# A gated cross-attention and expert layer: TensorE's first nine matmuls of constants left out

## Chip, core and metric

The kernel runs on one core of a Trainium2 chip. The metric is the device time of one execution in microseconds (us). The kernel is written by hand: every engine has its own program in a fixed order, and engines wait for each other by semaphores.

## What is computed

x is 4 sequences of 256 tokens, 256 wide (float32). Two steps, cut to the core:

```python
x = x + tanh(g_xattn[0]) * expert_forward(layernorm(x), gate_up_weight, down_weight)
x = x + tanh(g_ffn[0]) * ffn(layernorm(x), w_gate, w1, w2)

def smooth_quant_linear(x, w):            # int8 product; maxima per column, then per row
    s = sqrt(max(abs(x), axis=0) / max(abs(w), axis=0))
    xs, ws = x / s, w * s
    x_scale, w_scale = rowmax(abs(xs)) / 127, rowmax(abs(ws)) / 127
    return round(xs / x_scale) @ round(ws / w_scale).T * x_scale * w_scale.T
def expert_forward(x, guw, dw):           # once for each of the 4 sequences
    gate, up = split(smooth_quant_linear(x, guw))
    return smooth_quant_linear(silu(gate) * up, dw)
# ffn: each token goes to the best of 8 experts, 128 places each:
#   out = combine(gelu(dispatched @ w1[e]) @ w2[e]), w1[e] 256x1024, w2[e] 1024x256
```

## The kernel before

There are two stages. In the first (to some 55 us) the four sequences b = 0 to 3 go through the quantised layer, staggered over the engines. In the second the eight experts run one after another.

At the start, SyncE issues the loads of x (`load_x`) and of the gate and up weights cw (`load_cw`) in the order x0, x1, cw0, x2, cw1, x3, cw2, cw3. What follows for one sequence:

- VectorE takes the row statistics of x (`stats1`), GpSimd makes the reciprocal deviation (`rstd1`), ScalarE normalises (`norm1`) into `rows_w`.
- TensorE turns the weights (`turn1w(b)`, four 128x128 float32 transposes of cw[b], line 1019) and the normalised rows (`turn1(b)`, four transposes of rows_w, the same line). Both write to the PSUM tile bk[b], one half each.
- VectorE takes column maxima out of PSUM: `amax1w(b)` (line 715) of the turned weights, `amax1(b)` (lines 721 to 725) of the turned rows, and their ratio. GpSimd makes the scales from it with a power (`root_1(b)`, lines 368 and 370).
- ScalarE scales (`scale1`, line 531), TensorE turns back (`turn2`, line 1048), VectorE takes row maxima (`scales1`, line 740), ScalarE quantises, GpSimd rounds, TensorE turns (`turn3`, bfloat16 transposes of `ints`, line 1084) and multiplies.

Once, between `turn1(1)` and `turn1w(3)`, TensorE runs `mean_w` (line 1070, the column means of w_gate, four records in the trace), and VectorE centres with it (`centre_w`, line 780, tile wgc). VectorE's program has `amax1w(2)`, `amax1(1)`, `amax1(2)` behind `centre_w`, and TensorE's `turn1w(3)` waits for wgc.

`fill(b, a, n)` (line 1010) runs n bfloat16 matmuls of constants (`upper` against `identb`, 512 columns) into a half of a PSUM tile bk[b]. Nothing reads what they leave there: the next step that uses the half writes it anew. They stand in seven places of TensorE's program: 6 ahead of `turn1w(0)`, 3 ahead of `turn1w(1)`, 2 ahead of `turn2(0, 1)`, 4 ahead of `turn2(1, 1)`, and 6, 2 and 2 later in the first stage (25 in all). All have line 1013 in the trace. Transposes have one record each; a float32 matmul that is no transpose has two.

In the second stage TensorE works through `hidden` (line 1182) and `expert_out` (lines 1194 and 1196).

Of the kernel before, what the change touches and what calls it, by code (L numbers as in the profile page):

```python
# [5 lines left out]
def gated_smoothquant_moe_kernel(nc, x_in, ctx_in, down_in, g_xattn, g_ffn, w_gate, w1, w2, scratch, out):  # L6
# [20 lines left out]
    B, T, D = x_in.shape  # L27
    I = down_in.shape[2]
    E, _, F = w1.shape
    J = T // P  # L30
    K = D // P
# [14 lines left out]
    with ctx:  # L46
# [960 lines left out]
        def _(pe):  # L1007
            pe.wait_ge(consts, 4)

            def fill(b, a, n):  # L1010

                for _ in range(n):
                    nc.tensor.matmul(bk[b][:, a, :], upper[:], identb[:].unsqueeze(1).to_broadcast([P, 4, P]),  # L1013
                                     start=True, stop=True)
# [8 lines left out]
            def turn1w(b):  # L1023

                pe.wait_ge(cw_here[b], 16)
                if b == B - 1:
                    pe.wait_ge(wgc_ready, 1)
                turn1_half(b, 1, cw).then_inc(t1w_ready, 1)
# [185 lines left out]
                                           start=(n == 0), stop=(n == NF - 1))  # L1214
                ins.then_inc(y_used, 1)

            fill(3, 0, 6)
            turn1w(0)
            fill(3, 0, 3)
            turn1w(1)  # L1220
            turn1(0)
            turn1w(2)
# [96 lines left out]
```

## Time and profile before

| | us |
|---|---|
| median of 3 runs | 116.8 (116.26 to 116.91) |
| the profiled execution | 117.76 |
| its span, first to last instruction | 116.0 |
| around the span | 1.76 |
| TensorE matmul busy | 98.6 (85% of the span) |
| VectorE busy | 86.7 (75%) |
| ScalarE busy | 72.3 (62%) |
| GpSimd busy | 56.0 (48%) |
| share of the chain that ended last on TensorE, GpSimd, VectorE | 50%, 16%, 14% |

Start times below count from the first instruction. Matmul records overlap each other: the pace of a group is read from the distance between starts, not from the duration of one. "x4" behind a row means that four instructions are merged into it, and its duration runs from the first's start to the last's end.

### The profile page before, as it was taken

The numbers are of one execution on the slowest core, as the hardware profiler recorded it, in microseconds if no ns is written. First come the engines' busy times: TensorE is split into PE (matmuls) and PEld (weight loads), VectorE is DVE, ScalarE is ACT, GpSimd is POOL, SyncE is SP. The second block draws the span as 40 slices with busy tenths as digits, with TensorE's granted clock in tenths as the row PEclk, the third lists the DMA queues.
The fourth block names the chain that finished last, engine by engine and source line by source line (L and its number), as shares of the span: only waits on it lengthen the run. The fifth ranks groups of instructions, "written<-read, shape, count | busy, mean of one in ns | idle before, by whom it ended". The sixth has DMA issues, their size and how long they took to land.

```text
span 116.0 us, 2229 instructions
## 1 busy us (share of the span) xinstructions
PE 98.6 (85%) x741; PEld 84.4 (73%) x741; DVE 86.7 (75%) x231; ACT 72.3 (62%) x154; POOL 56.0 (48%) x119
## 2 busy tenths in 40 slices
PE   0948868997986898996889999999999999999930
PEld 0227546996845667874689989899999989899820
DVE  6646897999997889682318698999898696939450
ACT  4073579798797899966018564998573739376000
POOL 7855598787969849878670000426030303011041
PEclk9999999999999999999999999999999999999998
DMA  3899998999990942409932999989898860101011
GB/s 108 255 353 291 240 172 291 323 363 353 378 328 26 292 149 94 160 25 237 346 103 66 292 398 353 309 214 408 303 330 280 298 236 10 45 0 51 0 45 45
DMA packets 16218, 24.86 MB, mean 214 GB/s; under 512 B 1368, under 2 KB 13913, under 8 KB 15184
## 3 DMA queue, kind: packets, MB, share of 16 engines
q1 hardware_dynamic: 15440, 22.65, 62.1%
q0 software_dynamic: 768, 2.08, 4.8%
q8 instruction: 6, 0.10, 0.3%
q14 instruction: 4, 0.03, 0.1%
HBM read 20.50 MB, written 4.28 MB: 214 GB/s over the span
## 4 chain that ended last, share of the span: by engine, by line
PE 50%; POOL 16%; DVE 14%; issue 6%; DMA 6%; SPq 2%; ACT 2%; POOLq 1%
PE bk L1182 25%; PE bk L1194 11%; PE bk L1196 6%; DMA cw<-in_ctx_gu 6%; POOL slot_rows L426 4%; POOL row L412 2%; DVE am L740 2%; PE bk L1168 2%; POOL sc L370 2%; DVE am L786 2%; PE bk L1155 2%; PE bk L1208 2%; PE bk L1019 1%; SPq L231 1%; DVE am L721 1%
## 5 line engine op out<-in xcount | busy, mean ns | idle before, releaser
L494 POOL DMA_INDIRECT out<-scrow,gr x8 | 9.5, 1182 | 43.1 <-DVE scrow L961 41.7
L1182 PE MATMUL bk<-rows_w,w_sb 128*128 128x128 f32 x192 | 23.0, 275 | 0.5 <-ACT rows_w L583 0.5
L1182 PEld LDWEIGHTS bk<-rows_w,w_sb 128*128 128x128 f32 x192 | 22.2, 192 | 0.8 <-ACT rows_w L583 0.7
L1194 PE MATMUL bk<-w2p,hh 128*128 128x512 f32 x56 | 20.3, 403 | 0.0
L862 DVE TENSOR_TENSOR w2p<-w_sb,w2p 128x1024 fp32r<-128x1024 f32 x12 | 14.1, 1217 | 3.8 <-POOL begun L482 2.7
L1196 PE MATMUL bk<-w2p,hl 128*128 128x256 f32 x56 | 15.6, 278 | 0.0
L597 ACT ACTIVATE w2p<-w_sb 128x1024 fp32r<-128x1024 f32 x12 | 12.0, 1054 | 5.3 <-PE bk L1196 5.3
L661 ACT ACTIVATE hh<-bk 128x512 fp32r<-128x512 f32 x16 | 9.5, 595 | 4.7 <-PE bk L1182 4.7
L1194 PEld LDWEIGHTS bk<-w2p,hh 128*128 128x128 f32 x56 | 10.5, 188 | 2.1
L1196 PEld LDWEIGHTS bk<-w2p,hl 128*128 128x128 f32 x56 | 10.5, 188 | 0.0
L874 DVE TENSOR_TENSOR hl<-wide_a,hh 128x512 fp32r<-128x512 f32 x16 | 10.4, 683 | 0.0
L1013 PE MATMUL bk<-identb,upper 128*128 128x512 bf16 x25 | 7.8, 438 | 3.0 <-POOL upper L308 3.0
L426 POOL DMA_INDIRECT slot_rows<-row,slot x8 | 8.7, 1090 | 2.9 <-issue 2.9
L663 ACT ACTIVATE wide_a<-bk 128x512 f32<-128x512 f32 x16 | 9.6, 598 | 0.0
L1155 PE MATMUL bk<-row,wide_b 128*128 128x258 f32 x32 | 7.9, 391 | 1.8 <-POOL row L415 1.8
L1155 PEld LDWEIGHTS bk<-row,wide_b 128*128 128x128 f32 x32 | 5.8, 190 | 2.9 <-issue 2.2
L531 ACT ACTIVATE wide_a<-bk,sc 128x256 f32<-128x256 f32 x14 | 5.4, 482 | 2.3 <-POOL sc L370 2.3
L513 ACT ACTIVATE rows_w<-x,sh,rs 128x256 f32<-128x256 f32 x6 | 3.3, 593 | 5.3 <-POOL sh L333 5.3
L540 ACT ACTIVATE wide_b<-bk,q1r 128x256 f32<-128x256 f32 x16 | 6.4, 494 | 0.0
L1013 PEld LDWEIGHTS bk<-identb,upper 128*128 128x128 bf16 x25 | 2.5, 107 | 5.0 <-POOL upper L308 3.0
L1048 PE MATMUL bk<-ident,wide_a 128*128 128x128 f32 x32 | 4.5, 281 | 1.0 <-ACT wide_a L531 0.9
L1048 PEld LDWEIGHTS bk<-ident,wide_a 128*128 128x128 f32 x32 | 3.4, 140 | 2.5 <-ACT wide_a L531 2.4
(164 smaller groups left out, 229.9 us busy)
## 6 DMA issues: line engine op xcount, KB each, us to landing
w_sb<-in_w SPq DMA_DIRECT2D x12, 1024.0 KB, 7.4
slot_rows<-empty SPq DMA_DIRECT2D x1, 1068.0 KB, 9.9
x<-in_x SPq DMA_DIRECT2D x4, 256.0 KB, 4.3
cw<-in_ctx_gu SPq DMA_DIRECT2D x4, 256.0 KB, 6.3
cw<-in_w SPq DMA_DIRECT2D x1, 1024.0 KB, 7.1
out<-row SPq DMA_DIRECT2D x4, 256.0 KB, 2.6
x<-in_w SPq DMA_DIRECT2D x1, 1024.0 KB, 5.8
wide_a<-in_w SPq DMA_DIRECT2D x1, 1024.0 KB, 6.7
```

The costliest lines, as they stand in the source:

```text
L426: nc.gpsimd.indirect_dma_start(scratch, bass.IndirectOffsetOnAxis(ap=slot[:, b, j:j + 1], axis=0), row[:, b, j, 0:ROW], None, bounds_check ...
L494: nc.gpsimd.indirect_dma_start(out_rows, bass.IndirectOffsetOnAxis(ap=gr[:, e, TOKEN:TOKEN + 1].bitcast(I32), axis=0), yo[:, e % 2, :], No ...
L597: last = nc.scalar.activation(w2p[:, e % 2, n:n + NF // 2, 0], w2v[:, n:n + NF // 2], ACT.Copy)
L661: nc.scalar.activation(hh[:, e % 2, part].rearrange("p n c -> p (n c)"), HB[e % 2][:, m, :], ACT.Gelu_apprx_tanh).then_inc(hhigh_ready, 1)
L663: nc.scalar.activation(hs[:, e % 2, part].rearrange("p n c -> p (n c)"), HB[e % 2][:, m, :], ACT.Gelu_apprx_tanh).then_inc(gelu_ready, 1)
L862: last = nc.vector.tensor_tensor(w2p[:, e % 2, part, 1], w2v[:, part], w2p[:, e % 2, part, 0].bitcast(F32), ALU.subtract)
L874: nc.vector.tensor_tensor(hl[:, e % 2, part], hs[:, e % 2, part], hh[:, e % 2, part].bitcast(F32), ALU.subtract).then_inc(hlow_ready, 1)
L1013: nc.tensor.matmul(bk[b][:, a, :], upper[:], identb[:].unsqueeze(1).to_broadcast([P, 4, P]), start=True, stop=True)
L1155: ins = nc.tensor.matmul(XD[e], hot[:, b, j, e * C:(e + 1) * C], row[:, b, j, 0:RSTD + 1], start=(b == 0 and j == 0), stop=(b == B - 1 and ...
L1182: ins = nc.tensor.matmul(HB[e % 2][:, m, n * C:(n + 1) * C], wv[:, k, o:o + P], xgT[:, e % B, k], start=(k == 0), stop=(k == K - 1))
L1194: nc.tensor.matmul(YB[e % 2], hh[:, e % 2, n], w2p[:, e % 2, n].rearrange("p a d -> p (a d)"), start=(n == 0), stop=False)
L1196: ins = nc.tensor.matmul(YB[e % 2][:, 0:D], hl[:, e % 2, n], w2p[:, e % 2, n, 0], start=False, stop=(n == NF - 1))
```

## The change

The two calls of `fill` ahead of `turn1w(0)` and `turn1w(1)` are gone; the other 16 matmuls of constants stay. Nothing else differs.

```diff
-            fill(3, 0, 6)
             turn1w(0)
-            fill(3, 0, 3)
             turn1w(1)
             turn1(0)
             turn1w(2)
```

On TensorE, the start of the program. The names are bk for the PSUM tiles, identb and upper for the constants, cw for the gate and up weights, rows_w for the normalised rows, wide_a for the scaled ones. Before:

```order
0 L1006 UNCONDITIONAL_BRANCH
1 L1013 MATMUL bk<-identb,upper 128x512 x6
2 L1019 MATMUL bk<-ident,cw 128x128 x4
3 L1013 MATMUL bk<-identb,upper 128x512 x3
4 L1019 MATMUL bk<-ident,cw 128x128 x4
5 L1019 MATMUL bk<-ident,rows_w 128x128 x4
6 L1019 MATMUL bk<-ident,cw 128x128 x4
```

and now, with four rows more:

```order
0 L1006 UNCONDITIONAL_BRANCH
1 L1019 MATMUL bk<-ident,cw 128x128 x8
2 L1019 MATMUL bk<-ident,rows_w 128x128 x4
3 L1019 MATMUL bk<-ident,cw 128x128 x4
4 L1019 MATMUL bk<-ident,rows_w 128x128 x4
5 L1070 MATMUL bk<-wg,spread 128x8 x2
6 L1019 MATMUL bk<-ident,cw 128x128 x4
7 L1019 MATMUL bk<-ident,rows_w 128x128 x4
8 L1013 MATMUL bk<-identb,upper 128x512 x2
```

The turnings of cw[0] and cw[1] now follow each other as TensorE's first work; behind them the order is what it was. The other engines' programs are the same in both.

## Rows read from the trace of the kernel before

**Rows 1.** Chain that ended last: start us, us, what. From the weights' loads on.

```profile
3.65 6.48 DMA cw<-in_ctx_gu
...
10.18 1.09 PE bk L1019 x8
11.27 0.47 PE bk L1070 x4
...
11.77 0.17 DVE wgc L780
11.94 0.60 DVE am L715
...
14.13 1.02 POOL sc L370
...
19.49 0.64 PE bk L1019 x4
```

**Rows 2.** Timeline of TensorE's matmuls, 3 to 19 us; idle time and releaser in brackets.

```profile
3.01 2.74 PE L1013 MATMUL bk<-identb,upper 128*128 128x512 bf16 x6 [3.01 <-POOL upper L308]
5.78 0.66 PE L1019 MATMUL bk<-ident,cw 128*128 128x128 f32 x4
6.27 0.81 PE L1013 MATMUL bk<-identb,upper 128*128 128x512 bf16 x3
8.74 0.66 PE L1019 MATMUL bk<-ident,cw 128*128 128x128 f32 x4 [1.66 <-DMA cw<-in_ctx_gu]
9.23 0.60 PE L1019 MATMUL bk<-ident,rows_w 128*128 128x128 f32 x4
10.18 0.66 PE L1019 MATMUL bk<-ident,cw 128*128 128x128 f32 x4 [0.34 <-DMA cw<-in_ctx_gu]
...
11.12 0.61 PE L1070 MATMUL bk<-wg,spread 128*128 128x8 f32 x4
...
12.99 0.59 PE L1013 MATMUL bk<-identb,upper 128*128 128x512 bf16 x2
...
14.89 1.03 PE L1013 MATMUL bk<-identb,upper 128*128 128x512 bf16 x4
16.81 2.11 PE L1048 MATMUL bk<-ident,wide_a 128*128 128x128 f32 x16 [0.89 <-ACT wide_a L531]
```

**Rows 3.** Timeline of TensorE's weight loads inside the first six fills.

```profile
3.84 0.15 PEld L1013 LDWEIGHTS bk<-identb,upper 128*128 128x128 bf16 x1 [0.28 <-issue]
4.26 0.15 PEld L1013 LDWEIGHTS bk<-identb,upper 128*128 128x128 bf16 x1 [0.28 <-issue]
```

**Rows 4.** Timelines of VectorE and of GpSimd: the waits behind TensorE's first turnings.

```profile
6.47 0.69 DVE L715 TENSOR_REDUCE am<-bk 128x2 f32<-128x512 f32 x1 [1.37 <-PE bk L1019]
7.95 0.75 DVE L706 BATCH_NORM_STATS2 st<-x 128x6 f32<-128x256 f32 x2 [0.79 <-DMA x<-in_x]
...
11.77 0.17 DVE L780 TENSOR_TENSOR wgc<-wg,bk 128x16 f32<-128x16 f32 x1 [0.45 <-PE bk L1070]
...
13.83 0.22 POOL L368 TENSOR_SCALAR ra<-ra 128x2 f32<-128x2 f32 x1 [1.08 <-DVE ra L725]
```

**Rows 5.** Busy time of each engine in stretches, granted clock and DMA.

```profile
core 0: us, PE busy (x) PEld busy (x) DVE busy (x) ACT busy (x) POOL busy (x), PEclk, DMA share, GB/s
3.00:5.70 2.70, 2.69 (x6) 0.72 (x6) 1.82 (x8) 0.11 (x1) 2.39 (x9) 1.00 0.82 250
15.95:19.45 3.50, 2.11 (x16) 1.71 (x16) 3.38 (x10) 3.50 (x11) 3.01 (x8) 1.00 0.95 231
22.00:30.00 8.00, 7.28 (x73) 6.87 (x72) 7.69 (x26) 7.19 (x20) 6.90 (x15) 1.00 1.00 349
60.00:80.00 20.00, 20.00 (x162) 19.23 (x161) 16.92 (x30) 14.53 (x23) 3.47 (x4) 1.00 0.83 276
115.00:116.00 1.00, 0.00 (x0) 0.00 (x0) 0.00 (x0) 0.00 (x0) 0.00 (x0) 0.50 0.00 0
```

**Rows 6.** Timeline of TensorE: bfloat16 transposes of one sequence (turn3).

```profile
24.73 0.61 PE L1084 MATMUL bk<-identb,ints 128*128 128x128 bf16 x8
```

## The prediction

> **What bounds the kernel now.** I read the chain of waits first, because it says at which point TensorE's pace at the start begins to matter. Up to 10.13 us the chain is a transfer: cw[2] is issued at 3.65 and its landing releases TensorE [rows 1]. From there it is TensorE (eight transposes from 10.18, then `mean_w` from 11.27), VectorE (`centre_w` at 11.77, then the maxima), GpSimd's powers, and so on without another transfer. So whatever TensorE does before 8.7 us is free as long as it is done by then, and what it does from 10.18 to 11.7 is on the path that sets the end. The reader is to see two waits there: VectorE stood still 0.45 us for `mean_w`, and GpSimd 1.08 us for the ratio that VectorE makes after it [rows 4]. Neither has other work to slide in, since each program's order is fixed. In the second stage TensorE has no free time at all, 20.00 of 20 us [rows 5]; it can't win back a late start.
>
> Then the timeline of TensorE. The fills that go are the six from 3.01 and the three from 6.27 [rows 2]. They end, by these rows, at 5.75 and 7.08; the work behind them starts at 5.78 and 8.74.
>
> Last the clock. The granted clock reads 1.00 from 3.00 to 5.70 [rows 5], but the rows of the fills speak against that reading for this stretch: their weight loads stand 0.42 us apart [rows 3], which for 512 columns is the lower level, 1.2 GHz. From 6.27 on the fills are at the higher: four take 1.03 us and two 0.59 [rows 2], so one more costs (1.03 - 0.59) / 2 = 0.22 us. Between them the clock went from 1.2 to 2.4 GHz, with TensorE at work back to back since 3.01. I take 5.7 us for it, since the four transposes at 5.78 need 0.49 us to the next start, exactly as the four at 8.74 do (to 9.23).
>
> **The change part by part.**
>
> *The fills' own time.* 2.74 + 0.81 = 3.55 us of TensorE's work goes [rows 2]. All of it lies beside transfers: behind the last fill TensorE waits 1.66 us for cw[1]. Value: 0. If the first six did hold up `turn1w(0)`, the reader of it, VectorE, would start earlier than 6.47, but it waits 0.79 us for x[2] before 7.95 anyway [rows 4]. Still 0.
>
> *`turn1w(0)` at the lower clock.* Four transposes take 0.49 us at the higher level. No row shows a transpose at the lower one. The fills there take 0.42 against 0.22, a factor of 1.9; the other bound is a factor of 1, if something else than the array's clock paces a transpose. I take nearly the full factor, 0.24 for 0.1225, because the bfloat16 transposes follow the higher clock: eight take 0.61 us in all, at most 0.076 each [rows 6], less than the 0.107 that 128 columns take at 1.2 GHz. `turn1w(0)` then ends some 0.5 us later; VectorE's idle 0.79 us ahead of x[2] covers it. Cost 0. Without that cover it would cost 0.5.
>
> *`turn1w(1)`, `turn1(0)`, `turn1w(2)`, `turn1(1)`, `mean_w`.* With the fills gone, TensorE has done only four transposes when it comes to 8.74, and stood idle for 2 us behind them, so I expect it at 1.2 GHz there. Sixteen transposes lead up to `mean_w`. Before, they took from 8.74 to 11.12 with waits for transfers of 0.34 us among them. At the lower clock TensorE is behind the transfers and doesn't wait: 8.74 + 16 x 0.24 = 12.58. That is 1.46 us later than 11.12. `mean_w` itself, 0.47 us on the chain [rows 1], has four weight loads and few columns: between 0 and another 0.47. With no rise of the clock until then, the sum is 1.5 to 1.9 us.
>
> When does it rise? The earliest that I allow is with as much unbroken work behind it as in the trace, 3.01 to 5.7, thus 8.74 + 2.7 = 11.4. By then 2.7 / 0.24 = 11 transposes are done and 5 are left, 0.6 us: `mean_w` starts at 12.05, 0.9 us later. So the path at `centre_w` moves by 0.9 us (early rise) to 1.9 us (none yet). I take 1.3, a little under the middle of the two; the trace has one rise only, and nothing says that the next needs exactly as much.
>
> *What hangs on it.* VectorE goes from `centre_w` at 11.77 into `amax1w(2)` at 11.94 and on; GpSimd has waited 1.08 us for the ratio before its power at 14.13, and the chain leads by way of GpSimd to `turn1(3)` at 19.49 without a transfer [rows 1, 4]. With no transfer on it, I let the shift go through one to one. The two fills at 12.99 and the four at 14.89 each wait on TensorE's order only; if they run at the lower clock they cost 6 x 0.2 = 1.2 us more, ahead of `turn2(1, 1)` at 16.81, which now has 0.89 us of idle time in front [rows 2]. With a rise by about 12.5 that is none.
>
> Sum against the profiled execution: 117.76 + 0 + 0 + 1.3 = 119.1 us. The runs without a profile have a median of 116.8, 0.96 less; the same 1.3 gives **118.1 us**.
>
> A page speaks against a sum of this size. The Trainium skill, "TensorE: Matmul & The Clock Gate", Part 1, states that the array is at half rate by default and released by activity, and that the ramp's penalty is under 1% of a typical kernel's span. The first half fits the fills' spacing of 0.42 and then 0.22; by the second the change would cost under 1.2 us, against the 0.9 to 1.9 from the rows. I keep the rows, since this kernel is short and has the transposes on its path.
>
> **The rivals.**
>
> *Transposes don't raise the clock (late rise), 118.8 to 120.3.* If only products lift it, it stays low through `mean_w`'s few columns and past the transposes until the six fills left have run. Cost: 1.9 at `centre_w`, then `turn2(0)` and the fills at the lower level: from 13.0 the work of `turn1w(3)`, `turn1(2)`, two fills, `turn2(0)`, four fills is 16 x 0.24 + 6 x 0.42 = 6.4 us from about 14.0, to 20.4 against the 16.81 of before, less what the rise gives back on the way. 2 to 3.5 us in all, 118.8 to 120.3. Against it: from 15.95 to 19.45 TensorE does transposes alone and the clock stays at 1.00 [rows 5], while after the last matmul it is 0.50 at 115. That shows that they hold the clock, not that they raise it. The same page, Part 4, says that full clock does not engage for transpose mode; [rows 6] contradict it as to speed. Chance 0.18.
>
> *The clock stays low for much of the first stage, 121 to 124.* From 22 to 30 us TensorE is busy 7.28 of 8 us at the higher clock [rows 5]; at half of it, this stretch alone would add some 4 to 7 us. It decides if the fills that stay are too sparse to lift it. I see no reason why transposes and real products, nearly without a gap, should leave it low. Chance 0.06.
>
> *Not slower, 116.8 to 117.3.* The mechanism is the pace of a float32 transpose. If it is set by the weight load or by issue (each takes 0.1225 us where a bfloat16 one takes at most 0.076), the sixteen transposes keep their starts at either clock, TensorE still waits for cw[2], and all that is left is `mean_w`, up to 0.47 us. It decides at a pace of about 0.14 us: sixteen of these are 2.2 us, and `mean_w` could start at 11.12 as before. The same result comes if the clock is up by 8.74 all the same. Against it: the fills, whose pace did double, are matmuls like them, and the transposes of bfloat16 do run faster than 1.2 GHz allows. Chance 0.15.
>
> *Faster, below 116.2.* Fewer weight reads beside the first transfers could bring cw[2] in earlier; the constants are small and nothing in the trace shows such a contention. Chance 0.03.
>
> **How the numbers follow.** Forecast 0.58 (117.7 to 118.7), late rise 0.18, low for long 0.06, not slower 0.15, faster 0.03. The predicted time is the forecast's, 118.1. The range is 117.2 to 119.9: it takes in the forecast with both ends of its bounds and most of the late rise, and leaves out most of "not slower", "faster", the top of the late rise and "low for long", together about 0.2. A measurement of this kernel can tell 0.5%, 0.6 us, from no change. Slower by more than that: 0.58 + 0.18 + 0.06 less some 0.02 for small costs = 0.80; within it 0.17; faster 0.03.
>
> **What would show it right or wrong.** In the profile after: (1) the four transposes at about 5.8 and those at 8.74 have starts 0.24 us apart, not 0.12, and the granted clock reads 0.50 there or has no reading; (2) TensorE has no wait for cw[2] at 10.2; (3) `mean_w` starts between 12.0 and 12.6, and `centre_w` at 12.7 to 13.6 instead of 11.77; (4) GpSimd's power for b = 1 starts 0.9 to 1.9 us after 14.13; (5) the clock rises between 11.4 and 13, or else the fills behind 13 are 0.42 apart (late rise); (6) the first `hidden` starts later by the same amount. If the transposes are still 0.12 apart at 8.74 the forecast is wrong, and "not slower" is right. If (1) to (4) hold but the end moves by much less than `centre_w` does, then "one to one" was the wrong step.

## Result and profile after

Slower, by less than forecast. In the first comparison the changed kernel has a median of 117.38 us against 116.69 (20 runs each), a ratio of 1.0059 (95% interval 1.0035 to 1.0084). Two further comparisons gave 1.0086 (1.0048 to 1.0123) and 1.0079 (1.0045 to 1.0112). Over all its 38 executions the median is 117.52, over the 118 of before 116.67: 0.85 us or 0.7%, where 1.3 us was forecast and 117.2 to 119.9 stated as range. The spread grew as well: 111 of 118 executions of before are under 117.5 us, but 19 of 38 of the changed kernel.

The ratios leave out executions that are more than 1.5% above a kernel's fastest, so where many are left out the median of all of them stands beside the ratio.

The page of the changed kernel, against a span of 116.0 before:

```profile
span 115.2 us, 2212 instructions
PE 96.6 (84%) x732; PEld 85.0 (74%) x732; DVE 86.6 (75%) x231; ACT 72.3 (63%) x154; POOL 56.0 (49%) x119
PEclk9999999999999999999999999999999999999995
```

The profiled execution of the changed kernel is *shorter* than the one of before that the prediction stands on (116.94 against 117.76 us), though its median is longer. So a difference of two profiles alone would have told the wrong sign. TensorE's timeline tells why; these rows answer to [rows 2]:

```profile
5.86 1.09 PE L1019 MATMUL bk<-ident,cw 128*128 128x128 f32 x4 [5.86 <-DMA cw<-in_ctx_gu]
7.29 1.12 PE L1019 MATMUL bk<-ident,cw 128*128 128x128 f32 x4 [0.34 <-DMA cw<-in_ctx_gu]
8.20 1.06 PE L1019 MATMUL bk<-ident,rows_w 128*128 128x128 f32 x4
9.05 1.06 PE L1019 MATMUL bk<-ident,cw 128*128 128x128 f32 x4
9.91 0.65 PE L1019 MATMUL bk<-ident,rows_w 128*128 128x128 f32 x4
10.39 0.51 PE L1070 MATMUL bk<-wg,spread 128*128 128x8 f32 x4
```

Three things are to be seen. The four transposes of a group take 1.06 to 1.12 us where they took 0.60 to 0.66, and from one group to the next it is 0.85 us where it was 0.45 to 0.49. Taken singly, the starts of transposes in a row stand 0.213 us apart here, at the lower clock, and 0.109 us in before; only the first two of a group that follows a wait are farther apart (up to 0.27 and 0.17 us). In the fourth of the groups from 7.29 on this ends (0.65, and 0.48 to `mean_w`); the trace's first entry of a granted clock, at the full 2.4 GHz, is at 10.00 us. And the weights cw[1] were there at 7.3 us, not at 8.7; the wait for cw[2] (0.34 us in [rows 2]) is gone.

VectorE and GpSimd, answering to [rows 4]:

```profile
6.99 0.69 DVE L715 TENSOR_REDUCE am<-bk 128x2 f32<-128x512 f32 x1 [1.91 <-PE bk L1019]
7.59 0.74 DVE L706 BATCH_NORM_STATS2 st<-x 128x6 f32<-128x256 f32 x2
...
10.94 0.17 DVE L780 TENSOR_TENSOR wgc<-wg,bk 128x16 f32<-128x16 f32 x1 [0.35 <-PE bk L1070]
...
13.00 0.22 POOL L368 TENSOR_SCALAR ra<-ra 128x2 f32<-128x2 f32 x1 [0.99 <-DVE ra L725]
```

The first reduction is 0.52 us later than before and is hidden, as said: the statistics of x[2] follow it, at 7.59. `centre_w` still waits for TensorE, and GpSimd for VectorE.

The chain of waits, answering to [rows 1]; all sixteen transposes now stand in it as one piece:

```profile
2.66 4.58 DMA cw<-in_ctx_gu
...
7.29 3.26 PE bk L1019 x16
10.55 0.36 PE bk L1070 x4
...
10.94 0.17 DVE wgc L780
...
13.30 1.02 POOL sc L370
...
18.66 0.64 PE bk L1019 x4
```

From the start of `mean_w` to the end of the span it is 116.0 - 11.12 = 104.9 us in [rows 2], and 115.2 - 10.39 = 104.8 here. That quantity is the ruler of all that follows.

### The profile page after: what moved, and what is told of

It reads as the page before. It is cut to its first block, busy times and chain, and to the rows that moved or that the text cites. A ratio compares the mean times of both kernels' runs of the same rounds, so it can differ in the third digit from the quotient of the medians.

```text
span 115.2 us, 2212 instructions
## 1 busy us (share of the span) xinstructions
PE 96.6 (84%) x732; PEld 85.0 (74%) x732; DVE 86.6 (75%) x231; ACT 72.3 (63%) x154; POOL 56.0 (49%) x119
## 4 chain that ended last, share of the span: by engine, by line
PE 53%; POOL 16%; DVE 14%; issue 6%; DMA 4%; ACT 2%; SPq 1%; POOLq 1%
PE bk L1182 25%; PE bk L1194 11%; PE bk L1196 6%; POOL slot_rows L426 4%; DMA cw<-in_ctx_gu 4%; PE bk L1019 3%; POOL row L412 3%; DVE am L740 2%; PE bk L1168 2%; POOL sc L370 2%; DVE am L786 2%; PE bk L1155 2%; PE bk L1208 2%; DVE am L721 1%; POOL ints L398 1%
## 5 line engine op out<-in xcount | busy, mean ns | idle before, releaser
L1019 PE MATMUL bk<-ident,cw 128*128 128x128 f32 x16 | 3.9, 391 | 6.6 <-DMA cw<-in_ctx_gu 6.2
L1019 PEld LDWEIGHTS bk<-ident,cw 128*128 128x128 f32 x16 | 2.7, 201 | 7.0 <-issue 6.2
```

What stands on the lines that cost most here:

```text
L1019: ins = nc.tensor.transpose(bk[b][:, a, k * T + j * P:k * T + (j + 1) * P], src[:, b, j, k * P:(k + 1) * P], ident[:])
```

## Experiments

Each kernel was profiled once and timed beside the kernel before on the same chip. The table has what all of them gave; the rise is the first entry of 2.4 GHz in the trace's granted clock.

| kernel | cw[1] turned from | rise | `mean_w` at | span | span - `mean_w` | median (before) | ratio |
|---|---|---|---|---|---|---|---|
| before | 8.74 | 5.74 | 11.12 | 116.0 | 104.9 | 116.69 | |
| after | 7.29 | 10.00 | 10.39 | 115.2 | 104.8 | 117.38 (116.69) | 1.0059 |
| before_again | 7.67 | 8.62 | 9.89 | 114.8 | 104.9 | 116.63 (116.50) | 1.002 |
| after_again | 7.64 | 11.84 | 11.11 | 116.3 | 105.2 | 117.71 (116.50) | 1.0086 |
| before_third | 7.15 | 5.92 | 9.66 | 114.5 | 104.8 | 116.48 (116.66) | 0.9991 |
| after_third | 7.41 | 10.80 | 10.85 | 115.6 | 104.8 | 117.44 (116.66) | 1.0079 |
| no_six | 7.53 | 10.19 | 10.61 | 115.5 | 104.9 | 117.34 (116.50) | 1.0065 |
| no_three | 7.67 | 6.09 | 10.20 | 115.1 | 104.9 | 117.21 (116.50) | 1.0013 |
| narrow | 7.48 | 10.91 | 10.94 | 115.7 | 104.8 | 118.01 (116.56) | 1.0135 |
| early_ten | 7.41 | 5.26 | 9.97 | 114.9 | 104.9 | 116.64 (116.56) | 1.0006 |
| before_late | 8.67 | 11.97 | 12.03 | 116.8 | 104.8 | 117.46 (116.56) | 1.0078 |
| after_late | 7.95 | 17.03 | 11.42 | 116.9 | 105.5 | 118.59 (116.56) | 1.018 |
| before_swap | 7.67 | 7.62 | 10.15 | 114.6 | 104.4 | 116.58 (116.83) | 0.9983 |
| after_swap | 7.70 | 17.14 | 11.17 | 116.8 | 105.6 | 117.60 (116.83) | 1.0016 |
| early_ten_swap | 7.19 | 5.75 | 9.67 | 114.2 | 104.5 | 116.02 (116.66) | 0.9946 |
| no_fifteen | 7.09 | 9.96 | 10.27 | 115.8 | 105.5 | 118.14 (116.83) | 1.0135 |
| no_fills | 7.11 | 11.27 | 10.63 | 117.0 | 106.4 | 119.22 (116.83) | 1.0174 |

### The two kernels again

> The kernel before, run once more to see how its start differs between executions. Theory A (the transfers' landing differs by execution, whatever the fills do): the second transposes of gate and up weights need not start at 8.74 us; they start anywhere from 7.2 to 8.8, and mean_w accordingly at 9.9 to 11.2 us, still at 0.12 us a transpose. Theory B (the fills themselves keep the transfers back): again 8.6 to 8.8 us and a landing median of 6.3 us for cw. Ratio to the kernel before 1.000 by both.

> The changed kernel once more. Theory A: ratio to before 1.003 to 1.009 as measured, transposes from the second group on 0.21 us apart until the clock rises somewhere from 9.5 to 13 us; where the landings are late (8.7 us), mean_w starts later than the 10.39 us of the first profile, about 12 us. Theory B: landings early (7.3 us for cw[1]) once more, since the fills are gone.

before_again, TensorE's timeline:

```profile
3.00 2.74 PE L1013 MATMUL bk<-identb,upper 128*128 128x512 bf16 x6 [3.00 <-POOL upper L308]
5.54 1.06 PE L1019 MATMUL bk<-ident,cw 128*128 128x128 f32 x4
6.39 1.49 PE L1013 MATMUL bk<-identb,upper 128*128 128x512 bf16 x3
7.67 1.06 PE L1019 MATMUL bk<-ident,cw 128*128 128x128 f32 x4
8.53 0.65 PE L1019 MATMUL bk<-ident,rows_w 128*128 128x128 f32 x4
9.02 0.60 PE L1019 MATMUL bk<-ident,cw 128*128 128x128 f32 x4
9.45 0.60 PE L1019 MATMUL bk<-ident,rows_w 128*128 128x128 f32 x4
9.89 0.51 PE L1070 MATMUL bk<-wg,spread 128*128 128x8 f32 x4
```

Its chain of waits:

```profile
3.00 2.74 PE bk L1013 x6
5.75 0.85 PE bk L1019 x4
6.60 1.28 PE bk L1013 x3
7.88 0.87 PE bk L1019 x4
...
8.77 0.69 DVE am L715
```

This is the kernel *with* its fills, and the clock was still low at 7.67: the fills of 6.39 take 1.49 us instead of 0.81, and `turn1w(1)` 1.06. The rise comes at 8.62 here against 5.74 in the first profile, though TensorE's program to that point is the same. When the clock rises differs from execution to execution. And the three fills, slow, ended where `turn1w(1)` begins, without a wait for a transfer: they had held it back. The chain says the same of all nine: it starts with the constants and goes through the fills and `turn1w(1)` to VectorE, past `mean_w`, and `centre_w` at 10.57 had no wait in front. The groups at 9.02 and 9.45, at the higher clock, start 0.43 us apart: 0.109 us a transpose. So the landing fell where theory A put it, but not the "0.12 us a transpose" that came with it.

after_again, the same view:

```profile
7.64 1.12 PE L1019 MATMUL bk<-ident,cw 128*128 128x128 f32 x4 [1.40 <-DMA cw<-in_ctx_gu]
...
10.26 1.06 PE L1019 MATMUL bk<-ident,rows_w 128*128 128x128 f32 x4
11.11 0.86 PE L1070 MATMUL bk<-wg,spread 128*128 128x8 f32 x4
```

Here all sixteen transposes ran low, 3.47 us from 7.64 to 11.11, and `mean_w` took 0.86 instead of 0.51. The landings vary on both kernels. The loads of cw took 4.5 us in the median in before_again and 4.6 in before_third, with the fills, 4.8 to 5.2 us in the changed kernel's three profiles, without them, and 6.3 us in the first profile of before only. Theory B (the fills hold the transfers back) falls.

> The kernel before, a third profile. If the late landing of its first profile (second group of transposes at 8.74 us) was that execution's own, they start at 7.5 to 7.9 us here and mean_w at 9.8 to 10.3; if it belongs to the kernel, at 8.6 us or later.

> The changed kernel, a third profile and more times, to settle the size between the 0.7 and the 1.2 us of the two comparisons. By the terms as measured so far: second group at 7.1 to 7.7 us, mean_w 3.1 to 3.5 us later, 104.9 us from there to the end if the clock is up by then and up to 105.6 if not; median 0.7 to 1.2 us over before.

```profile
7.15 0.66 PE L1019 MATMUL bk<-ident,cw 128*128 128x128 f32 x4 [0.18 <-DMA cw<-in_ctx_gu]
7.65 0.60 PE L1019 MATMUL bk<-ident,rows_w 128*128 128x128 f32 x4
8.54 0.66 PE L1019 MATMUL bk<-ident,cw 128*128 128x128 f32 x4 [0.29 <-DMA cw<-in_ctx_gu]
...
9.66 0.52 PE L1070 MATMUL bk<-wg,spread 128*128 128x8 f32 x4
```

These are before_third's rows: high clock, cw[1] at 7.15, both earlier than expected. The first profile's 8.74 is the latest of the seventeen profiles, among those without an added transfer by 1.0 us: it belongs to that execution. after_third turned cw[1] at 7.41 and reached `mean_w` at 10.85, 3.44 us later, as expected.

### One group of fills at a time

```diff
-            fill(3, 0, 6)
             turn1w(0)
             fill(3, 0, 3)
```

> Only the six fills ahead of turn1w(0) left out; the three behind it stay. Clock theory: the three run at the lower clock, 0.43 us apart, to about 8.0 us, and the rise comes by 8 to 11 us, earlier than without all nine: between no cost and the full one, ratio 1.000 to 1.006; the fills may also hold the second transposes back by some 0.7 us where the weights land early. If the fills only kept transfers back, ratio below 1.000.

1.0065 (1.0041 to 1.0089), median 0.84 us over before: like the whole change, and just above the 1.006 that was expected at most. The three fills run low and end where `turn1w(1)` begins (this is no_six):

```profile
5.99 1.49 PE L1013 MATMUL bk<-identb,upper 128*128 128x512 bf16 x3
7.53 1.12 PE L1019 MATMUL bk<-ident,cw 128*128 128x128 f32 x4
```

```diff
             fill(3, 0, 6)
             turn1w(0)
-            fill(3, 0, 3)
```

> Only the three fills behind turn1w(0) left out; the six stay. Clock theory: in executions where the six have raised the clock it stays up over the idle time to 7.3 or 8.7 us and nothing is lost: ratio 0.999 to 1.003, transposes 0.12 us apart at the second group in most executions. If both groups were needed, the ratio is that of the whole change, 1.006.

The profile has the clock up (rise 6.09) and the groups at 7.67 and 8.16 start 0.49 us apart as at the higher clock, which is what the clock theory says. But the times fall into two lots: seven of twelve between 116.2 and 117.4 us, four at 118.2 to 118.5, and one far off (344). The ratio of 1.0013 (0.998 to 1.0046) leaves the second lot out; the median of all, 117.21, is 0.7 us above before. That six fills alone raise the clock in some executions only, and that the slow lot is the one where they missed, is likely from the sizes but not shown: the one profile is of the fast lot.

### Columns, or a place in the program

```diff
-            fill(3, 0, 6)
+            narrow(3, 0, 6)      # matmul(bk[b][:, a, 0:E], upper[:], identb[:, 0:E])
             turn1w(0)
-            fill(3, 0, 3)
+            narrow(3, 0, 3)
```

> The nine matmuls of constants stay in number and place but have 8 columns instead of 512, so that TensorE does next to nothing in the same places. Clock theory (the fills' columns raise the clock): like the changed kernel, ratio 1.005 to 1.009, the second transposes 0.21 us apart. Rival (what counts is that TensorE's program starts early or that instructions stand there): like the kernel before, ratio 1.000 to 1.002.

1.0135 (1.0091 to 1.0179) in six runs. Nine matmuls in the same places, but of 8 columns, bring nothing:

```profile
3.00 0.33 PE L1019 MATMUL bk<-identb,upper 128*128 128x8 bf16 x6 [3.00 <-POOL upper L308]
...
7.48 1.12 PE L1024 MATMUL bk<-ident,cw 128*128 128x128 f32 x4 [0.29 <-DMA cw<-in_ctx_gu]
```

The rival is out: it is the work of the fills that counts. The ratio is above the 1.005 to 1.009 expected, though the profile is that of a changed kernel (`mean_w` at 10.94). The six times fall into two lots, 117.34 to 117.54 and 118.48 to 118.92 us. The changed kernel has times in both too, but its fastest is 116.53, so that the ratio leaves out what lies above 118.3; here nothing is left out. That, and six runs only, may be all that the difference is.

### More fills, earlier

```diff
+            nc.vector.memset(ones[:], float(E)).then_inc(ones_ready, 1)   # VectorE's first instruction
-            pe.wait_ge(consts, 4)
-            fill(3, 0, 6)
+            pe.wait_ge(ones_ready, 1)
+            for _ in range(10):
+                nc.tensor.matmul(bk[3][:, 0, :], ones[:], ones[:].unsqueeze(1).to_broadcast([P, 4, P]),
+                                 start=True, stop=True)
+            pe.wait_ge(consts, 4)
```

> More heat, earlier: the six fills are replaced by ten of another constant that VectorE writes first, from about 1.2 us to 5.5 us; the three stay. Clock theory: the clock has risen by 6 us in more executions than before, none pays at the second transposes; median 0.1 to 0.4 us below the kernel before and a narrower spread, ratio 0.996 to 0.999, mean_w at 9.8 to 10.3 us. Rival (the kernel before loses nothing to the clock): 1.000.

1.0006 (0.9985 to 1.0026): no gain, where 0.996 to 0.999 was expected. The clock was up early (5.26), but then TensorE waits 0.19 and 0.38 us for cw[1] and cw[2] and `mean_w` starts at 9.97. With the clock up, the landings set its start, and before_again, low until 8.62, was there at 9.89 with earlier landings. What before loses to a late rise is too small to be seen in the median of these twelve runs.

### The landings

```diff
             load_cw(0)
+            sp.dma_start(w2_sb[:, 2, 0:J * D]..., x_in[0]...).then_inc(early_here, 16)
             load_x(2)
```

> The kernel before with one more transfer of 256 KB (read by nobody) ahead of x[2] and cw[1], so that they land some 0.7 us later, as in the first profile of before. The start of mean_w moves by as much, and the end with it: 0.5 to 1.0 us slower than before, ratio 1.004 to 1.009. If the end doesn't hang one to one on mean_w, less.

> The changed kernel with the same extra transfer. Theory A (late landings make the change dearer or cheaper): the difference to before_late is clearly other than the 0.7 to 1.2 us between the two without it. Theory C (the price hangs on sixteen transposes of 0.21 instead of 0.12 us and on when the clock rises, not on the landings): again 0.6 to 1.2 us over before_late, ratio to before 1.010 to 1.018.

The medians are 117.46 and 118.59, 0.90 us over before and 0.88 over after_again's 117.71. The difference between the two is 1.13 us, inside 0.6 to 1.2: in the medians, of six runs each, theory C holds and later landings move both alike. The two profiles don't show it: their spans are 116.8 and 116.9, and before_late's is its slowest execution. In it the three fills at the lower clock stood between a late cw[0] and `turn1w(1)` at 8.67, and all sixteen transposes ran nearly as slowly as in the changed kernel; nothing was left of the fills' gain. The two profiles are of use for the clock:

```profile
10.38 1.06 PE L1024 MATMUL bk<-ident,cw 128*128 128x128 f32 x4
11.23 0.96 PE L1024 MATMUL bk<-ident,rows_w 128*128 128x128 f32 x4
12.03 0.51 PE L1075 MATMUL bk<-wg,spread 128*128 128x8 f32 x4
```

These are before_late's: a kernel with all its fills whose clock rose at 11.97 only. after_late's rose at 17.03:

```profile
11.42 0.86 PE L1075 MATMUL bk<-wg,spread 128*128 128x8 f32 x4
12.64 1.09 PE L1024 MATMUL bk<-ident,cw 128*128 128x128 f32 x4 [0.35 <-DVE wgc L785]
```

Its span is 116.9 - 11.42 = 105.5 behind the start of `mean_w`, 0.6 us above the ruler. Of that 0.35 is `mean_w` itself; another five microseconds at the lower clock cost 0.3. So with VectorE's order as it is, the price of the clock is paid ahead of `mean_w`, and hardly behind it.

### Is VectorE's wait for mean_w on the path?

```diff
             amax1(0)
-            centre_w()
             amax1w(2)
+            centre_w()
             amax1(1)
```

> VectorE takes the maxima of the turned weights of sequence 2 (line 715) ahead of centre_w (line 780) instead of behind it; nothing else. If its wait of 0.45 us for mean_w is on the path that sets the end, the reduction fills that wait and all behind moves up by 0.3 to 0.6 us: ratio 0.995 to 0.998. If the path goes elsewhere: 1.000, or slower, since turn1w(3) waits longer for wgc.

> The same swap on the changed kernel. If the price of the change is paid through mean_w and centre_w, the swap takes 0.3 to 0.6 us off it as well: ratio to before 1.002 to 1.005 instead of 1.006 to 1.009. If the low clock is paid elsewhere (in turn2, or later), it stays at 1.006 to 1.009.

before_swap's profile shows it (VectorE), the reduction of line 715 now in what was a wait:

```profile
10.17 0.68 DVE L715 TENSOR_REDUCE am<-bk 128x2 f32<-128x512 f32 x1
10.80 0.17 DVE L780 TENSOR_TENSOR wgc<-wg,bk 128x16 f32<-128x16 f32 x1
10.89 0.68 DVE L721 TENSOR_REDUCE am<-bk 128x2 f32<-128x512 f32 x1
```

From `mean_w` to the end it is 104.4 instead of 104.9, some 0.4 us less. The times can't tell it by themselves (0.9983, 0.9956 to 1.0009). after_swap is undecided: a ratio of 1.0016 (0.9979 to 1.0053) without its four longest runs, a median 0.77 us over before with them. One of the four (118.54) is the profiled one. Its clock rose at 17.14 only, and 105.6 us lie behind `mean_w`, 1.2 more than in before_swap; after_late, with a rise as late, had 0.6 more than the ruler. The chain goes through TensorE all the way from `centre_w`, and six of the fills that stayed are on it:

```profile
12.38 1.94 PE bk L1019 x8
14.32 0.85 PE bk L1013 x2
15.18 1.71 PE bk L1048 x8
16.88 1.05 PE bk L1013 x4
```

With VectorE's wait filled, a low clock behind `mean_w` was no longer nearly free.

> Ten earlier fills of another constant and the swap of centre_w with the maxima of sequence 2 together. With the clock up by 6 us the start hangs on the landings and then on VectorE; the swap fills its wait: ratio 0.994 to 0.998. If the swap gave nothing in the kernel before, 1.000.

Both together gave a median of 116.02 against 116.66, 0.9946 (0.9922 to 0.9969), two runs far off left out: faster than both kernels. Its profile has again 104.5 us behind `mean_w` (114.2 - 9.67). Alone neither edit is clear of no change (1.0006 for the earlier fills, on another chip, and 0.9983 for the swap). With the 0.4 us that both profiles show, the wait is on the path, though how the gain divides between the two edits stays open.

### The fills that stayed

```diff
-            fill(3, 0, 2)
             turn2(0, 1)
             turn2(0, 0)
-            fill(3, 0, 4)
             turn2(1, 1)
```

(both on the changed kernel; no_fills leaves out the last ten as well)

> The changed kernel with the two fills ahead of turn2(0, 1) and the four ahead of turn2(1, 1) left out too. If the transposes raise the clock, these six are not needed: ratio as the changed kernel, 1.005 to 1.010, rise from 9.5 to 13.5 us in most executions. If transposes count little, the rise comes behind 17 us and the ratio is 1.010 to 1.030.

> All 25 matmuls of constants left out. If the clock, once up, holds through the first stage without them: as no_fifteen, within 0.002. If the later ten are what holds it, the clock falls between 35 and 55 us, and part of the first stage or the first expert runs at 1.2 GHz: 1 to 3 us more.

The rise came as without the change, at 9.96 and 11.27. But the clock fell again. Granted clock is the third value from the end; first no_fifteen, then no_fills:

```profile
10.00:16.70 6.70, 4.00 (x32) 3.23 (x31) 5.97 (x20) 4.83 (x13) 4.75 (x9) 1.00 1.16 206
16.90:20.10 3.20, 3.20 (x17) 2.98 (x16) 2.27 (x6) 3.08 (x9) 2.82 (x7) 0.50 0.98 335
```

```profile
35.20:38.50 3.30, 3.06 (x13) 2.65 (x14) 1.51 (x7) 1.68 (x6) 3.22 (x9) 0.50 0.27 72
```

Before the fall in no_fifteen, at 16.78, TensorE had turned sixteen tiles from 11.13 on with idle time among them, the last of it 1.74 us up to 15.85, and then some eight more. In no_fills it stood idle for 2.37 us at the same place and the clock stayed up; it fell at 35.16, in a gap of some 2 us where six of the fills had been. Afterwards it rose again, at 20.20 and 38.57.

The ratios are 1.0135 (1.0089 to 1.0182) and 1.0174 (1.011 to 1.0238), and the profiles have 0.7 and 1.5 us more behind `mean_w` than the ruler. So no_fifteen came out above the 1.005 to 1.010 expected, though its interval touches it, and no_fills took its second branch, a fall between 35 and 55 us. It is not only the profiled executions: the mean granted clock is 0.985 or less in three of six executions of no_fifteen and in five of six of no_fills; of the changed kernel's 38 executions none is under 0.988. So the fills that stayed help to keep the clock up.

## Why the prediction was right or wrong

**The clock is what the fills buy: right.** Signs (1) and (2) came: the transposes run slower from 5.8 us on, and the wait for cw[2] is gone. The granted clock has no reading of 0.50 before its first entry and shows 1.00 there, as in [rows 5]; the pace has to be read from the rows. Signs (3) to (6) were times set against the first profile of before, and missed: `mean_w` at 10.39, GpSimd's power at 13.30 and the first `hidden` at 57.70 (58.53 there) are *earlier* than there, and the clock rose at 10.00. Held against before_third (9.66), `mean_w` is later by 0.7 us. narrow shows that it is the fills' columns, not their place.

**A shift of mean_w goes through one to one: right.** Twelve profiles have VectorE's order unchanged and the later fills in place. In ten of them 104.8 or 104.9 us lie behind the start of `mean_w`, over starts from 9.66 to 12.03; in the two whose clock was still low there (after_again, after_late) it is 105.2 and 105.5. The six fills behind it cost nothing at either clock that these profiles had (0.3 us at most, in after_late). The rule has a floor that the prediction doesn't name: in before_again `mean_w` started early enough that VectorE came to `centre_w` without a wait. And it is shown for this order of VectorE's only: in after_swap 1.2 us were paid behind `mean_w`.

**turn1w(0) hidden: right.** Its reader moved by 0.52 us, and the idle time before x[2] took it.

**The size: wrong, 1.3 us instead of 0.85 (0.69 in the first comparison).** The step that failed is the price of the sixteen transposes: "8.74 + 16 x 0.24 = 12.58", and no rise allowed before 11.4. Measured, a transpose takes 0.213 us at the lower clock, and the rise came at 10.00 to 11.84. Four points of the sum were off.

- *The pace.* "I take nearly the full factor, 0.24 for 0.1225". The factor was right: 0.213 against 0.109 is 1.96, where the fills have 0.427 against 0.216. The 0.1225 was wrong. It is the mean of a group that follows a wait, whose first step is longer (0.17 us); the next group in [rows 2], from 10.67 to 11.12, already reads 0.45 us for four. Sixteen at the lower clock took 3.47 us (after_again) instead of 3.84. That alone takes 0.4 us off the "no rise" end: 3.47 against 2.38 from 8.74 to 11.12 is 1.1, not 1.46; with `mean_w`'s 0.35 (of "between 0 and another 0.47") the upper end is 1.4, not 1.9.
- *The rise.* I allowed nothing before 11.4. It came at 10.00, 10.80 and 11.84 in the three profiles, 2.7, 3.4 and 4.2 us after the second group's start; counted from that start, the earliest case that I allowed is the first of the three, but its time on the clock was wrong. The three profiles of the changed kernel need 3.10, 3.44 and 3.47 us for the sixteen. Against the 2.38 of before that is 0.7 to 1.1 us, and with up to 0.35 for `mean_w` 0.7 to 1.4, where the prediction had 0.9 to 1.9.
- *The base.* "Before, they took from 8.74": I took one execution's landings as the kernel's. In before_again and before_third `mean_w` starts at 9.89 and 9.66, 1.2 to 1.5 us earlier. By the medians of before_late and after_late it shifts both kernels alike and so costs the difference little, but it hid the next term, and it made a profile of 117.76 us out of a kernel of 116.7.
- *"Value: 0" for the fills' own time.* With weights landing at 7.1 to 7.7 us, three fills at the lower clock (1.49 us, before_again and no_six) end just where `turn1w(1)` begins. Where the fills miss the rise they are on the path, all nine of them in before_again's chain, and the changed kernel gets something back: it turned cw[1] from 7.29, 7.64 and 7.41, and before_again from 7.67. That is 0 to 0.4 us by these starts; how much it is in the mean isn't shown.

In starts of `mean_w`: 10.39, 11.11 and 10.85 in the changed kernel, against 9.89 and 9.66 where the weights weren't late. That is 10.78 - 9.78 = 1.0 us on the mean of so few profiles, against 0.85 in the medians of 38 and 118 executions. How often the fills of before miss the rise, and so how the 0.85 divides between executions, stays open: it would take many profiles of one kernel.

**The rivals.** *Transposes don't raise the clock*: out as a mechanism. Up to 10.00 us the changed kernel's TensorE had done nothing but transposes, and the clock rose. That speaks against the Trainium skill, "TensorE: Matmul & The Clock Gate", Part 4, where full clock is said not to engage for transpose mode. The same page of the Trainium skill, in Part 1, has the ramp's penalty under 1% of a typical kernel's span; the three comparisons agree, with 0.6 to 0.9%. But a late rise as this rival describes it does happen. In after_late and after_swap the clock rose at 17.03 and 17.14 only, when two of the fills that stayed had run, 0.43 us apart, and the other four had begun. With the 1.1 us of the sixteen transposes that makes some 1.7 us in after_late, less than the rival's 2 to 3.5. That the changed kernel's four longest executions (118.35 to 118.71 us) are such ones is likely, but none of them was profiled. Against this rival the prediction also said that transposes hold the clock. That was more than its row could show: in no_fifteen, with transposes and gaps only behind `mean_w`, it fell. *Low for much of the first stage*: not with the fills that stayed; a first step of it shows when they go (no_fifteen, no_fills). *Not slower* by the pace of a transpose: out, the pace nearly doubles, as the fills' does. *Faster*: out; the loads of cw took no less time without the fills.

## What to carry to other kernels

A warm-up of TensorE is worth the work that would otherwise run at half the clock on the path, and no more: here sixteen transposes by 0.104 us, less the wait for a transfer in which the faster pace ends (0.34 us in [rows 2]) and less what a rise midway gives back. Price it from the first transfer that releases real work to the first point where another engine waits for TensorE; behind that point, five microseconds at the lower clock cost 0.3 us here. That depends on what fills the other engine's wait: in after_swap, with the wait filled, a rise as late cost about twice as much behind that point (1.2 us against 0.6, `mean_w` itself included). Take the pace of an instruction from a run of them in a row, not from a group of four behind a wait. And where a kernel begins on transfers, take two or three profiles before one execution's landing times go into a sum: here they differed by more than the change was worth.

## What the runs showed of the hardware

- The clock's rise is not fixed to the program. With the same instructions it came at 5.74, 5.92 and 8.62 us (three profiles of before), and in before_late, with six fills from 3.00, at 11.97. In the three profiles of the changed kernel the execution's time goes with it: rise at 10.00, 10.80, 11.84 us, time 116.94, 117.38, 118.07 us. The landings of cw[1] differ too (7.29, 7.41, 7.64), by 0.35 of the 1.1 us; the rest goes with the rise. Some of what looks like noise in the runs is likely this.
- A clock once up can fall in a stage in which TensorE still works but with gaps, and rise again: 0.50 in the row 16.90 to 20.10 of no_fifteen and in the row 35.20 to 38.50 of no_fills.
- Float32 transposes in a row start 0.109 us apart at the higher and 0.213 at the lower clock, a factor of 1.96, like the 512-column fills with 0.216 and 0.427 (before and before_again). The first step behind a wait is longer, up to 0.17 and 0.27 us, so that a group of four takes up to 0.49 and 0.91 us.
